# New instruction orders on TensorE, ScalarE and VectorE in a fused layernorm, linear attention and FFN kernel

## The chip, the cores and the metric

The kernel runs on one core of a Trainium2 chip. The metric is the device time of one execution in microseconds (us). Three executions of the kernel before took 555.29, 557.46 and 555.6 us, median 555.6 us. All times in the text are us unless marked ns.

## The reference

The input x has 8 batches of 1024 tokens with 256 channels. The output is x + attention + FFN, both of the layernorm of x:

```
xn  = layernorm(x)
q, k, v = split(xn @ qkv_w + qkv_b), 16 heads of 16 channels
q = q / |q| ; k = k / |k|            (per token and head)
kv  = sum over tokens of k^T v       (16x16 per head)
att = (q @ kv) @ proj_w + proj_b
ffn = relu(xn @ W1 + b1) @ W2 + b2   (1024 hidden channels)
out = x + att + ffn
```

## The kernel before

All matrix products are done in three passes of rounded float32: each operand is held as a rounded high part and a low part (the rest), and a product is high x high, high x low, low x high. So every operand costs a high part (a copy, mostly on ScalarE: functions *_high) and a low part (a subtraction, mostly on VectorE: *_low; for the normalised rows on GpSimd: split_xn).

A batch b is two halves of 512 tokens, s = 2b (even) and 2b + 1 (odd). In a half, TensorE runs the FFN as eight pairs ffn_up(s, u, j) (512 columns, six matmuls, into w_bank[j % 2]) and ffn_down(s, b, u, j) (six matmuls of 512 columns into o_bank). I call each such group of six a unit. ffn_up(j) may start when h_low(j - 2) has emptied its bank; ffn_down(j) needs h_low(j). h_high(s, j) on ScalarE and h_low(s, j) on VectorE turn the bank into the two parts of the hidden rows.

Between the units stand the products of attention, most of them short (256 or 128 columns): gather (xn^T k, eight matmuls of 512 columns and eight of 256), key_value, project, and the query-key product of the next half. That is done for two tile pairs n = 0, 1 in four steps, qk_begin (six matmuls of 256), qk_second (six), qk_third (six), qk_fourth (three), with fewer products in all than the plain form. Between the steps ScalarE and VectorE pass partial sums on: qk_seed on ScalarE (two copies of 256 columns; it waits for qk_begin and for both outputs of the pair before, qk_pair_out), qk_seed on VectorE (needed by qk_third), qk_sum on VectorE (needed by qk_fourth). qk_pair_out (a square and a copy) empties the banks; its second call for a pair waits for qk_fourth. Then sum_pair_squares, bound, qk_root and norms give 1/|q|, 1/|k|; divide(1, u) scales k and divide(0, u) scales q, and the high and low parts follow. At the end of a batch attend multiplies q with the batch's matrix m (m_high, m_low), and yT_out, add_attention, spread_y and GpSimd's add_rows build the output rows.

Transposes go by VectorE in 32x32 blocks (transpose_x, transpose_q) and then by 16 DMAs that SyncE issues (move). When the x blocks of half s + 1 have landed (x_moved), GpSimd forms three sums of them (x_forms, lines 445, 449 and 452; they are the input of the query-key steps), and ScalarE copies them (xT_high).

Each engine works through its own list in order; the lists are written out by hand: second_half (the odd half of batch 0), even_half and odd_half (batches 1 to 6 and the even half's and odd half's order in a loop), last_even_half and last_odd_half (batch 7). Engines meet by semaphores only. An instruction that waits holds up all that stands behind it in its list. The odd half's first TensorE units before are up 2, up 3, down 0, down 1, down 2, up 4.

Of the kernel before, what the change touches and what calls it, by code (L numbers as in the profile page):

```python
# [66 lines left out]
def build(nc, x, qkv_w, qkv_b, proj_w, proj_b, w1, b1, w2, b2, out):  # L67
# [6 lines left out]
    with ctx:  # L74
# [895 lines left out]
        def _(dve):  # L970
# [340 lines left out]
            def even_half(b, s):  # L1311
# [62 lines left out]
            def last_even_half(b, s):  # L1374
                h_low(s, 2)
                xT_low(s + 1, 1)
                x_forms_low(s + 1)
# [6 lines left out]
                h_low(s, 5)
                transpose_q(s, 0)
                k_low(s, 0)
                h_low(s, 6)
                qk_seed(s + 1, 1)
# [508 lines left out]
```

## Time and profile before

| | before |
|---|---|
| median of three executions | 555.6 us (555.29 to 557.46) |
| the profiled execution, its span | 555.33 us, 553.6 us |
| granted TensorE clock | 1.00 of full speed all along |
| TensorE busy | 546.7 us (99%), 2824 matmuls |
| weight loads busy | 466.2 us (84%) |
| VectorE, ScalarE, GpSimd busy | 441.4 us (80%), 311.6 us (56%), 188.4 us (34%) |

The page's busy time of TensorE counts each matmul from its start to its modelled end; they overlap, so the distance from start to start is what counts for the time. In the timelines each line has the start and the duration in us.

### The profile page before, as it was taken

To read this page: it belongs to the slowest core of one execution; us is meant where nothing else is said; L and a number is where in the kernel's file an instruction comes from. 1 tells how busy PE (TensorE), PEld (TensorE's weight loads), DVE (VectorE), ACT (ScalarE), POOL (GpSimd) and SP (SyncE) were. 2 spreads that over 40 slices of the span, in tenths; PEclk is the share of its full clock that TensorE was granted. 3 is DMA by queue.
4 is the path that set the end of the run, shared out by engine and by line. 5 is a ranking of instruction groups with operands and counts; after the bars stand their busy time and mean duration, and the time that the engine had idled before them with its cause. 6 is when DMAs were issued, how large, how long until landed. Compare 5 with 4: busy or idle time off the path is not lost.

```text
span 553.6 us, 9454 instructions
## 1 busy us (share of the span) xinstructions
PE 546.7 (99%) x2824; PEld 466.2 (84%) x2824; DVE 441.4 (80%) x856; ACT 311.6 (56%) x594; POOL 188.4 (34%) x196
## 2 busy tenths in 40 slices
PE   9999999999999999999999999999999999999997
PEld 7888878878888788887988888888888888888896
DVE  6977799687896878879698697977879778785745
ACT  4686644674636665475744757547484473743520
POOL 4242678140370304622146222442226331270010
PEclk9999999999999999999999999999999999999999
DMA  8522134351432525135251352413524133140633
GB/s 260 167 84 50 38 85 88 79 108 42 103 61 76 108 71 106 23 78 109 71 100 29 79 108 71 92 38 81 105 71 85 38 72 79 36 78 18 136 76 78
DMA packets 141416, 45.37 MB, mean 82 GB/s; under 512 B 133331, under 2 KB 136403, under 8 KB 141397
## 3 DMA queue, kind: packets, MB, share of 16 engines
q1 hardware_dynamic: 139280, 44.61, 35.1%
q10 hardware_dynamic: 2116, 0.53, 0.5%
q8 instruction: 9, 0.15, 0.1%
q14 instruction: 11, 0.08, 0.1%
HBM read 20.98 MB, written 8.39 MB: 53 GB/s over the span
## 4 chain that ended last, share of the span: by engine, by line
PE 88%; DVE 8%; issue 2%; ACT 1%; DVEq 0%
PE o_bank L1453 11%; PE o_bank L1454 10%; PE o_bank L1455 10%; PE w_bank L1453 9%; PE w_bank L1454 9%; PE w_bank L1455 9%; PE v_bank L1453 6%; PE v_bank L1455 6%; PE v_bank L1454 6%; DVE w_raw L1145 4%; PE g_bank L1629 3%; PE kv_bank L1629 3%; DVE h_lo L1159 1%; PE kv_bank L1634 1%; PE g_bank L1634 1%
## 5 line engine op out<-in xcount | busy, mean ns | idle before, releaser
L719 ACT ACTIVATE h_hi<-w_bank 128x512 fp32r<-128x512 f32 x128 | 75.9, 599 | 89.7 <-PE w_bank L1455 89.6
L438 POOL TENSOR_TENSOR xn_lo<-xn,xn_hi 128x256 fp32r<-128x256 f32 x56 | 42.1, 751 | 191.8 <-ACT xn_hi L598 187.6
L1453 PE MATMUL w_bank<-xT_hi,w_hi 128*128 128x512 f32 x254 | 100.1, 394 | 0.0
L1454 PE MATMUL w_bank<-xT_lo,w_hi 128*128 128x512 f32 x254 | 99.4, 391 | 0.0
L1455 PE MATMUL w_bank<-xT_hi,w_lo 128*128 128x512 f32 x254 | 99.0, 390 | 0.0
L1453 PE MATMUL o_bank<-h_hi,w_hi 128*128 128x512 f32 x240 | 94.9, 395 | 1.4 <-DVE h_lo L1159 1.4
L1454 PE MATMUL o_bank<-h_lo,w_hi 128*128 128x512 f32 x240 | 94.1, 392 | 0.0
L1455 PE MATMUL o_bank<-h_hi,w_lo 128*128 128x512 f32 x240 | 93.4, 389 | 0.0
L1159 DVE SCALAR_TENSOR_TENSOR h_lo<-w_bank,h_hi 128x512 fp32r<-128x512 f32 x128 | 86.2, 682 | 6.5 <-ACT h_hi L719 4.1
L486 POOL TENSOR_TENSOR y_sb<-y_sb,y_rows 128x256 f32<-128x256 f32 x56 | 63.3, 1135 | 13.8 <-DVE y_rows L1203 10.5
L1455 PEld LDWEIGHTS w_bank<-xT_hi,w_lo 128*128 128x128 f32 x254 | 47.7, 188 | 10.5
L1453 PEld LDWEIGHTS w_bank<-xT_hi,w_hi 128*128 128x128 f32 x254 | 47.8, 188 | 9.7 <-DVE h_lo L1159 1.2
L1453 PEld LDWEIGHTS o_bank<-h_hi,w_hi 128*128 128x128 f32 x240 | 45.3, 189 | 11.3 <-DVE h_lo L1159 4.0
L1454 PEld LDWEIGHTS w_bank<-xT_lo,w_hi 128*128 128x128 f32 x254 | 47.9, 188 | 8.0
L1455 PEld LDWEIGHTS o_bank<-h_hi,w_lo 128*128 128x128 f32 x240 | 45.1, 188 | 9.9
L1454 PEld LDWEIGHTS o_bank<-h_lo,w_hi 128*128 128x128 f32 x240 | 45.3, 189 | 7.0
L1126 DVE TENSOR_REDUCE qk_v<-qk_sq 128x32 f32<-128x512 f32 x52 | 35.2, 676 | 12.7 <-ACT qk_sq L700 12.7
L445 POOL TENSOR_TENSOR xn<-xT_raw 128x512 f32<-128x512 f32 x13 | 18.2, 1400 | 64.1 <-DMA xT_raw<-blocks 64.1
L1116 DVE TENSOR_TENSOR v_bank<-v_bank,qk_fifth 128x256 f32<-128x256 f32 x26 | 11.2, 432 | 34.2 <-PE v_bank L1455 34.2
L625 ACT ACTIVATE xn<-x_sb,ln_offset,ln_rstd 128x256 f32<-128x256 f32 x52 | 27.0, 591 | 20.2 <-DVE ln_offset L1034 20.2
L700 ACT ACTIVATE qk_sq<-v_bank 128x512 f32<-128x512 f32 x52 | 31.0, 595 | 9.1 <-DVE v_bank L1121 6.5
L1145 DVE TENSOR_TENSOR w_raw<-w_raw,qk_rn 128x1024 f32<-128x1024 f32 x16 | 25.6, 1631 | 0.1
(246 smaller groups left out, 1253.5 us busy)
## 6 DMA issues: line engine op xcount, KB each, us to landing
y_rows<-blocks SPq DMA_DIRECT2D x256, 32.0 KB, 1.9
x_sb<-x SPq DMA_DIRECT2D x15, 512.0 KB, 3.4
y_sb<-x SPq DMA_DIRECT2D x60, 128.0 KB, 3.2
out<-y_sb SPq DMA_DIRECT2D x58, 128.0 KB, 2.5
xT_raw<-blocks SPq DMA_DIRECT2D x224, 32.0 KB, 1.9
y_sb<-w SPq DMA_DIRECT2D x4, 256.0 KB, 5.3
x_sb<-x SPq DMA_DIRECT2D x2, 256.0 KB, 3.0
w_raw<-w SPq DMA_DIRECT2D x2, 256.0 KB, 7.4
```

Source lines behind the costliest of these rows:

```text
L438: nc.gpsimd.tensor_tensor(xn_lo[:, u, t, :], xn_of(s)[:, t, :], xn_hi[:, u, t, :].bitcast(F32), ALU.subtract).then_inc(xn_split_done, 1)
L486: nc.gpsimd.tensor_tensor(y_sb[:, u, t, :], y_sb[:, u, t, :], y_rows[:, u, t, :], ALU.add).then_inc(y_done, 1)
L625: done = nc.scalar.activation(to[:, t, :], x_sb[:, u, t, :], ACT.Identity, bias=ln_offset[:, t:t + 1], scale=ln_rstd[:, t:t + 1])
L700: nc.scalar.activation(qk_sq[:, w, :], v_bank[w][:], ACT.Square).then_inc(qk_sq_done, 1)
L719: nc.scalar.activation(h_hi[:, j % RING, :], w_bank[j % 2][:], ACT.Relu).then_inc(h_done, 1)
L1126: nc.vector.tensor_reduce(to, qk_sq[:, w, :].rearrange("p (w h d) -> p w h d", w=2, d=D), AXIS.X, ALU.add).then_inc(qk_ss_done, 1)
L1145: nc.vector.tensor_tensor(part, part, by, ALU.mult).then_inc(done, 1)
L1159: nc.vector.scalar_tensor_tensor(h_lo[:, r, :], w_bank[j % 2][:], 0.0, h_hi[:, r, :].bitcast(F32), ALU.max, ALU.subtract).then_inc(h_lo_do ...
L1453: nc.tensor.matmul(to, left[0], right[0], start=first, stop=False, skip_group_check=shared)
L1454: nc.tensor.matmul(to, left[0], right[1], start=False, stop=False, skip_group_check=shared)
L1455: return nc.tensor.matmul(to, left[1], right[0], start=False, stop=last, skip_group_check=shared)
L1629: nc.tensor.matmul(g_banks[k][:], xn_hi[:, u, t, k * P:(k + 1) * P], k_parts[:, t].rearrange("p w n -> p (w n)"), start=u == 0 and t == 0, ...
```

## The change

Only the order of the calls in the hand-written lists of TensorE, ScalarE and VectorE changes, in second_half, even_half, odd_half, last_even_half and last_odd_half. No instruction is added or taken away, no size, wait or buffer is changed, and GpSimd's and SyncE's lists stay as they are. In the odd half TensorE's first units become up 2, down 0, down 1, up 3, up 4, down 2; in the even half up 2, down 0, down 1, up 3, down 2, up 4. The short groups come side by side more often (gather with qk_begin, qk_fourth with qk_begin, key_value between qk_second and qk_third). The diff, function by function, with the calls alone (the two lists of the last batch, changed in the same way, are left out):

```diff
# scalar: second_half
...
+h_high(1, 3)
 xn_high(2, 0)
-h_high(1, 3)
+ln_root(3)
 k_high(1, 1)
-ln_root(3)
+qk_out(2, 0, 0)
+qT_high(0, 0)
+qk_out(2, 0, 1)
 normalise(3, 1)
+g_high(0)
 h_high(1, 4)
-qk_out(2, 0, 0)
+qk_out(2, 0, 2)
+h_high(1, 5)
 xn_high(3, 1)
-qT_high(0, 0)
-h_high(1, 5)
-g_high(0)
-qk_out(2, 0, 1)
 h_high(1, 6)
-qk_out(2, 0, 2)
 h_high(1, 7)
-qT_high(1, 1)
 qk_out(2, 0, 3)
 h_high(2, 0)
+qT_high(1, 1)
 m_high(0)
# scalar: even_half
...
 h_high(s, 4)
-h_high(s, 5)
 qk_seed(s + 1, 0)
 ln_root(s + 2)
+h_high(s, 5)
 normalise(s + 2, 0)
 qk_pair_out(s + 1, 1, 0, 0)
+xn_high(s + 2, 0)
 qk_pair_out(s + 1, 1, 0, 1)
 qk_seed(s + 1, 1)
+qT_high(s, 0)
 h_high(s, 6)
 h_high(s, 7)
-qT_high(s, 0)
-xn_high(s + 2, 0)
 qk_pair_out(s + 1, 1, 1, 0)
 qk_pair_out(s + 1, 1, 1, 1)
+h_high(s + 1, 0)
 qk_root(s + 1)
-h_high(s + 1, 0)
-h_high(s + 1, 1)
 yT_out(b, 0, 0)
 yT_out(b, 0, 1)
+h_high(s + 1, 1)
 xT_high(s + 2, 0)
# scalar: odd_half
...
 g_high(b)
-qk_seed(s + 1, 0)
 ln_root(s + 2)
 h_high(s, 4)
+qk_seed(s + 1, 0)
 h_high(s, 5)
...
 qk_pair_out(s + 1, 0, 0, 0)
+h_high(s, 6)
+xn_high(s + 2, 1)
 qk_pair_out(s + 1, 0, 0, 1)
 qk_seed(s + 1, 1)
-xn_high(s + 2, 1)
-h_high(s, 6)
-qT_high(s, 1)
 h_high(s, 7)
...
 qk_pair_out(s + 1, 0, 1, 0)
+qk_pair_out(s + 1, 0, 1, 1)
 h_high(s + 1, 0)
-qk_pair_out(s + 1, 0, 1, 1)
+qk_root(s + 1)
+qT_high(s, 1)
 h_high(s + 1, 1)
-qk_root(s + 1)
 xT_high(s + 2, 1)
# vector: second_half
...
 transpose_q(1, 1)
+sum_squares(2, 0)
 h_low(1, 3)
+transpose_x(3)
 h_low(1, 4)
-g_low(0)
-transpose_x(3)
-h_low(1, 5)
-sum_squares(2, 0)
-h_low(1, 6)
 sum_squares(2, 1)
 qT_low(0, 0)
+h_low(1, 5)
+g_low(0)
 sum_squares(2, 2)
+h_low(1, 6)
 mask_kv(0)
...
 sum_squares(2, 3)
+m_low(0)
 bound(2)
 h_low(2, 0)
-m_low(0)
 h_low(2, 1)
# vector: even_half
...
 transpose_q(s, 0)
+xT_low(s + 1, 1)
+h_low(s, 3)
 x_forms_low(s + 1)
-h_low(s, 3)
-xT_low(s + 1, 1)
 variance(s + 2, b + 1, 0)
+h_low(s, 4)
+spread(s + 2)
 qk_seed(s + 1, 0)
-spread(s + 2)
-h_low(s, 4)
+qk_sum(s + 1, 0)
+transpose_x(s + 2)
 h_low(s, 5)
-qk_sum(s + 1, 0)
 sum_pair_squares(s + 1, 0, 0)
-transpose_x(s + 2)
+qk_seed(s + 1, 1)
 sum_pair_squares(s + 1, 0, 1)
-qk_seed(s + 1, 1)
 h_low(s, 6)
+h_low(s, 7)
+qk_sum(s + 1, 1)
 qT_low(s, 0)
-qk_sum(s + 1, 1)
-h_low(s, 7)
 sum_pair_squares(s + 1, 1, 0)
...
 h_low(s + 1, 0)
+divide(1, 1, k_done)
 h_low(s + 1, 1)
-divide(1, 1, k_done)
# vector: odd_half
...
 divide(0, 1, q_done)
+h_low(s, 2)
 transpose_q(s, 1)
-h_low(s, 2)
 k_low(s, 1)
+xT_low(s + 1, 0)
+h_low(s, 3)
 x_forms_low(s + 1)
-h_low(s, 3)
-xT_low(s + 1, 0)
 variance(s + 2, b + 1, 1)
+spread(s + 2)
 g_low(b)
+qk_seed(s + 1, 0)
 h_low(s, 4)
-qk_seed(s + 1, 0)
-spread(s + 2)
 h_low(s, 5)
 qk_sum(s + 1, 0)
+mask_kv(b)
 transpose_x(s + 2)
-mask_kv(b)
+sum_pair_squares(s + 1, 0, 0)
+h_low(s, 6)
+sum_pair_squares(s + 1, 0, 1)
 qk_seed(s + 1, 1)
-h_low(s, 6)
+h_low(s, 7)
 qk_sum(s + 1, 1)
-sum_pair_squares(s + 1, 0, 0)
-h_low(s, 7)
-sum_pair_squares(s + 1, 0, 1)
 m_low(b)
-qT_low(s, 1)
 sum_pair_squares(s + 1, 1, 0)
-h_low(s + 1, 0)
 sum_pair_squares(s + 1, 1, 1)
 bound(s + 1)
+h_low(s + 1, 0)
 norms(s + 1)
+qT_low(s, 1)
 h_low(s + 1, 1)
# tensor: second_half
...
 ffn_up(1, 1, 2)
+ffn_down(1, 0, 1, 0)
 ffn_up(1, 1, 3)
-ffn_down(1, 0, 1, 0)
 query_key(2, 0, 0)
+query_key(2, 0, 1)
 ffn_down(1, 0, 1, 1)
-query_key(2, 0, 1)
 ffn_up(1, 1, 4)
...
 gather(1, 0, 1)
+query_key(2, 0, 2)
 ffn_up(1, 1, 5)
...
 ffn_down(1, 0, 1, 3)
-query_key(2, 0, 2)
+ffn_up(1, 1, 7)
 ffn_down(1, 0, 1, 4)
-ffn_up(1, 1, 7)
 key_value(0)
+query_key(2, 0, 3)
+ffn_up(2, 0, 0)
 ffn_down(1, 0, 1, 5)
-ffn_up(2, 0, 0)
-query_key(2, 0, 3)
-ffn_down(1, 0, 1, 6)
 project(0)
 ffn_up(2, 0, 1)
+ffn_down(1, 0, 1, 6)
 ffn_down(1, 0, 1, 7)
# tensor: even_half
...
 ffn_up(s, 0, 2)
-ffn_up(s, 0, 3)
 ffn_down(s, b, 0, 0)
 ffn_down(s, b, 0, 1)
+ffn_up(s, 0, 3)
+ffn_down(s, b, 0, 2)
 ffn_up(s, 0, 4)
 gather(s, b, 0)
+qk_begin(s + 1, 1, 0, b)
 ffn_up(s, 0, 5)
-qk_begin(s + 1, 1, 0, b)
-ffn_down(s, b, 0, 2)
 qk_second(s + 1, 1, 0)
+ffn_up(s, 0, 6)
+qk_third(s + 1, 0)
 ffn_down(s, b, 0, 3)
-qk_third(s + 1, 0)
-ffn_up(s, 0, 6)
+ffn_down(s, b, 0, 4)
 qk_fourth(s + 1, 1, 0)
+qk_begin(s + 1, 1, 1, b)
 ffn_up(s, 0, 7)
-qk_begin(s + 1, 1, 1, b)
-ffn_down(s, b, 0, 4)
 qk_second(s + 1, 1, 1)
...
 qk_third(s + 1, 1)
+ffn_up(s + 1, 1, 0)
+qk_fourth(s + 1, 1, 1)
 ffn_down(s, b, 0, 6)
-qk_fourth(s + 1, 1, 1)
-ffn_up(s + 1, 1, 0)
 ffn_up(s + 1, 1, 1)
# tensor: odd_half
...
 ffn_up(s, 1, 2)
-ffn_up(s, 1, 3)
 ffn_down(s, b, 1, 0)
 ffn_down(s, b, 1, 1)
+ffn_up(s, 1, 3)
+ffn_up(s, 1, 4)
 ffn_down(s, b, 1, 2)
-ffn_up(s, 1, 4)
 gather(s, b, 1)
 qk_begin(s + 1, 0, 0, b)
+ffn_up(s, 1, 5)
 ffn_down(s, b, 1, 3)
-ffn_up(s, 1, 5)
 qk_second(s + 1, 0, 0)
+key_value(b)
+qk_third(s + 1, 0)
 ffn_up(s, 1, 6)
-qk_third(s + 1, 0)
+ffn_up(s, 1, 7)
+qk_fourth(s + 1, 0, 0)
+qk_begin(s + 1, 0, 1, b)
 ffn_down(s, b, 1, 4)
-qk_fourth(s + 1, 0, 0)
-key_value(b)
-qk_begin(s + 1, 0, 1, b)
-ffn_up(s, 1, 7)
 qk_second(s + 1, 0, 1)
...
 qk_fourth(s + 1, 0, 1)
+ffn_up(s + 1, 0, 1)
 ffn_down(s, b, 1, 6)
-ffn_up(s + 1, 0, 1)
 ffn_down(s, b, 1, 7)
...
```

## Rows read from the trace of the kernel before

**Rows 1.** List of waits, TensorE: total us, times, longest.
```profile
PE o_bank L1453 <- DVE h_lo L1159: 1.4, 6, 0.3
```

**Rows 2.** Timeline of TensorE around a gather: short and long products.
```profile
263.17 0.28 PE L1453 MATMUL v_bank<-wqk_hi,xT_hi 128*128 128x256 f32 x1
...
263.89 0.40 PE L1453 MATMUL o_bank<-h_hi,w_hi 128*128 128x512 f32 x1
...
265.28 0.39 PE L1453 MATMUL w_bank<-xT_hi,w_hi 128*128 128x512 f32 x1
...
266.64 0.28 PE L1453 MATMUL v_bank<-wqk_forms_hi,xf_hi 128*128 128x256 f32 x1
```

**Rows 3.** Timeline of TensorE at the start of an odd half: start, duration, line, operation.
```profile
251.61 0.44 PE L1453 MATMUL w_bank<-xT_hi,w_hi 128*128 128x512 f32 x1
253.05 0.39 PE L1453 MATMUL w_bank<-xT_hi,w_hi 128*128 128x512 f32 x1
...
256.90 0.39 PE L1455 MATMUL o_bank<-h_hi,w_lo 128*128 128x512 f32 x1
257.53 0.50 PE L1453 MATMUL o_bank<-h_hi,w_hi 128*128 128x512 f32 x1 [0.24 <-DVE h_lo L1159]
...
259.02 0.40 PE L1453 MATMUL w_bank<-xT_hi,w_hi 128*128 128x512 f32 x1
```

**Rows 4.** Timeline of VectorE there: last of norms, h_low 0 and 1, both divides, h_low 2.
```profile
250.38 0.29 DVE L983 SCALAR_TENSOR_TENSOR qk_rn<-qk_e,qk_y 128x128 f32<-128x128 f32 x1
250.81 1.29 DVE L1159 SCALAR_TENSOR_TENSOR h_lo<-w_bank,h_hi 128x512 fp32r<-128x512 f32 x2
252.01 3.45 DVE L1145 TENSOR_TENSOR w_raw<-w_raw,qk_rn 128x1024 f32<-128x1024 f32 x2
...
256.82 0.65 DVE L1159 SCALAR_TENSOR_TENSOR h_lo<-w_bank,h_hi 128x512 fp32r<-128x512 f32 x1
```

**Rows 5.** Timeline of the weight loads there.
```profile
251.55 0.19 PEld L1453 LDWEIGHTS w_bank<-xT_hi,w_hi 128*128 128x128 f32 x1 [0.20 <-DVE h_lo L1159]
```

**Rows 6.** VectorE's block transposes of x, even half before rows 3.
```profile
240.11 1.30 DVE L1068 STREAM_TRANSPOSE blocks<-xn 128x512 f32<-128x512 f32 x2
```

**Rows 7.** Timeline of ScalarE, same half: yT_out twice.
```profile
251.13 1.40 ACT L733 ACTIVATE xn_first<-o_bank,bias_T 128x512 f32<-128x512 f32 x2
```

**Rows 8.** Timeline of ScalarE: qk_seed's two copies; the last copy of qk_pair_out.
```profile
241.84 0.37 ACT L598 ACTIVATE v_bank<-v_bank 128x256 f32<-128x256 f32 x1 [0.91 <-PE v_bank L1455]
242.12 0.38 ACT L598 ACTIVATE qk_fifth<-v_bank 128x256 f32<-128x256 f32 x1
...
248.20 0.59 ACT L598 ACTIVATE w_raw<-v_bank 128x512 f32<-128x512 f32 x1
```

**Rows 9.** TensorE: the qk_fourth whose result that last copy takes.
```profile
247.15 0.28 PE L1453 MATMUL v_bank<-wqk_forms_hi,xT_hi 128*128 128x256 f32 x1
```

**Rows 10.** The divide's line, one of its two forms: duration in ns, least, median, most.
```profile
L1145 DVE TENSOR_TENSOR w_raw<-w_raw,qk_rn x16: 1211/1220/2327, 53.7 to 523.2; 128x1024 f32<-128x1024 f32 x16
```

**Rows 11.** Timeline of GpSimd in the stretch of rows 3.
```profile
253.07 1.31 POOL L445 TENSOR_TENSOR xn<-xT_raw 128x512 f32<-128x512 f32 x1 [4.17 <-DMA xT_raw<-blocks]
254.46 1.60 POOL L449 TENSOR_TENSOR xn<-xT_raw,xn 128x256 f32<-128x256 f32 x1
```

**Rows 12.** SyncE's moves of x in the even half before rows 3.
```profile
241.43 10.28 SPq L372 DMA_DIRECT2D xT_raw<-blocks  x16
```

**Rows 13.** TensorE at the end of batch 0: attend starts late.
```profile
82.01 0.47 PE L1453 MATMUL v_bank<-qT_hi,m_hi 128*128 128x512 f32 x1 [0.83 <-issue]
```

**Rows 14.** VectorE there: bound, h_low, m_low, and qT_low.
```profile
78.47 2.24 DVE L1132 TENSOR_SCALAR qk_v<-qk_v 128x128 f32<-128x128 f32 x1
...
81.24 0.67 DVE L973 TENSOR_TENSOR m_lo<-g_bank,m_hi 128x512 fp32r<-128x512 f32 x1
...
83.40 1.23 DVE L973 TENSOR_TENSOR qT_lo<-y_rows,qT_hi 128x1024 fp32r<-128x1024 f32 x1
```

**Rows 15.** GpSimd there: the low parts of the weight forms.
```profile
78.24 2.40 POOL L471 TENSOR_TENSOR wqk_forms_lo<-wvp_raw,wqk_forms_hi 128x1024 fp32r<-128x1024 f32 x1
```

More of the change, by code:

```diff
@@ L898, in odd_half @@
                 qk_pair_out(s + 1, 0, 1, 0)
+                qk_pair_out(s + 1, 0, 1, 1)
                 h_high(s + 1, 0)
-                qk_pair_out(s + 1, 0, 1, 1)
+                qk_root(s + 1)
+                qT_high(s, 1)
                 h_high(s + 1, 1)
-                qk_root(s + 1)
                 xT_high(s + 2, 1)
             def last_even_half(b, s):
+                x_forms_high(s + 1)
                 h_high(s, 2)
+                h_high(s, 3)
+                qk_seed(s + 1, 0)
+                h_high(s, 4)
+                h_high(s, 5)
                 k_high(s, 0)
-                x_forms_high(s + 1)
-                h_high(s, 3)
-                h_high(s, 4)
-                qk_seed(s + 1, 0)
-                h_high(s, 5)
                 qk_pair_out(s + 1, 1, 0, 0)
+                h_high(s, 6)
                 qk_pair_out(s + 1, 1, 0, 1)
-                h_high(s, 6)
+                qk_seed(s + 1, 1)
                 h_high(s, 7)
-                qk_seed(s + 1, 1)
+                qk_pair_out(s + 1, 1, 1, 0)
                 h_high(s + 1, 0)
-                qk_pair_out(s + 1, 1, 1, 0)
                 qk_pair_out(s + 1, 1, 1, 1)
                 qk_root(s + 1)
-                h_high(s + 1, 1)
                 qT_high(s, 0)
                 yT_out(b, 0, 0)
+                h_high(s + 1, 1)
                 yT_out(b, 0, 1)
@@ L931, in last_odd_half @@
                 h_high(s, 4)
+                g_high(b)
                 h_high(s, 5)
-                g_high(b)
+                m_high(b)
                 h_high(s, 6)
-                m_high(b)
                 qT_high(s, 1)
@@ L1315, in even_half @@
                 transpose_q(s, 0)
+                xT_low(s + 1, 1)
+                h_low(s, 3)
                 x_forms_low(s + 1)
-                h_low(s, 3)
-                xT_low(s + 1, 1)
                 variance(s + 2, b + 1, 0)
+                h_low(s, 4)
+                spread(s + 2)
                 qk_seed(s + 1, 0)
-                spread(s + 2)
-                h_low(s, 4)
+                qk_sum(s + 1, 0)
+                transpose_x(s + 2)
                 h_low(s, 5)
-                qk_sum(s + 1, 0)
                 sum_pair_squares(s + 1, 0, 0)
-                transpose_x(s + 2)
+                qk_seed(s + 1, 1)
                 sum_pair_squares(s + 1, 0, 1)
-                qk_seed(s + 1, 1)
                 h_low(s, 6)
+                h_low(s, 7)
+                qk_sum(s + 1, 1)
                 qT_low(s, 0)
-                qk_sum(s + 1, 1)
-                h_low(s, 7)
                 sum_pair_squares(s + 1, 1, 0)
@@ L1374, in last_even_half @@
             def last_even_half(b, s):
+                xT_low(s + 1, 1)
                 h_low(s, 2)
-                xT_low(s + 1, 1)
+                h_low(s, 3)
                 x_forms_low(s + 1)
-                h_low(s, 3)
+                divide(0, 0, q_done)
+                h_low(s, 4)
                 qk_seed(s + 1, 0)
-                h_low(s, 4)
-                divide(0, 0, q_done)
+                h_low(s, 5)
                 qk_sum(s + 1, 0)
+                transpose_q(s, 0)
+                h_low(s, 6)
+                h_low(s, 7)
+                qk_seed(s + 1, 1)
                 sum_pair_squares(s + 1, 0, 0)
[L1384 to L1388, printed above, removed]
                 qk_sum(s + 1, 1)
                 sum_pair_squares(s + 1, 0, 1)
-                h_low(s, 7)
+                k_low(s, 0)
                 sum_pair_squares(s + 1, 1, 0)
@@ L1396, in last_even_half @@
                 h_low(s + 1, 0)
+                divide(1, 1, k_done)
                 h_low(s + 1, 1)
-                divide(1, 1, k_done)
                 qT_low(s, 0)
@@ L1403, in last_odd_half @@
                 divide(0, 1, q_done)
+                k_low(s, 1)
+                transpose_q(s, 1)
                 h_low(s, 3)
-                transpose_q(s, 1)
-                k_low(s, 1)
+                h_low(s, 4)
                 g_low(b)
-                h_low(s, 4)
                 mask_kv(b)
@@ L1412, in last_odd_half @@
                 m_low(b)
+                qT_low(s, 1)
                 h_low(s, 7)
-                qT_low(s, 1)
             def half(b, s, u, last):
@@ L1810, in last_even_half @@
                 ffn_up(s, 0, 2)
+                ffn_up(s, 0, 3)
                 ffn_down(s, b, 0, 0)
-                ffn_up(s, 0, 3)
                 ffn_down(s, b, 0, 1)
+                ffn_down(s, b, 0, 2)
+                qk_begin(s + 1, 1, 0, b)
                 ffn_up(s, 0, 4)
-                qk_begin(s + 1, 1, 0, b)
-                ffn_down(s, b, 0, 2)
+                ffn_down(s, b, 0, 3)
                 qk_second(s + 1, 1, 0)
@@ L1819, in last_even_half @@
                 qk_third(s + 1, 0)
-                ffn_down(s, b, 0, 3)
-                qk_fourth(s + 1, 1, 0)
                 ffn_up(s, 0, 6)
                 ffn_up(s, 0, 7)
+                qk_fourth(s + 1, 1, 0)
                 qk_begin(s + 1, 1, 1, b)
                 ffn_down(s, b, 0, 4)
+                ffn_up(s + 1, 1, 0)
+                qk_second(s + 1, 1, 1)
                 ffn_down(s, b, 0, 5)
-                qk_second(s + 1, 1, 1)
+                qk_third(s + 1, 1)
                 ffn_down(s, b, 0, 6)
-                qk_third(s + 1, 1)
-                ffn_up(s + 1, 1, 0)
                 qk_fourth(s + 1, 1, 1)
+                ffn_up(s + 1, 1, 1)
                 gather(s, b, 0)
-                ffn_up(s + 1, 1, 1)
                 ffn_down(s, b, 0, 7)
@@ L1837, in last_odd_half @@
                 ffn_up(s, 1, 2)
-                ffn_up(s, 1, 3)
                 ffn_down(s, b, 1, 0, True)
                 ffn_down(s, b, 1, 1, True)
+                ffn_up(s, 1, 3)
                 ffn_up(s, 1, 4)
-                ffn_up(s, 1, 5)
                 gather(s, b, 1)
                 ffn_down(s, b, 1, 2, True)
+                ffn_up(s, 1, 5)
+                ffn_up(s, 1, 6)
+                key_value(b)
                 ffn_down(s, b, 1, 3, True)
-                key_value(b)
-                ffn_up(s, 1, 6)
                 ffn_down(s, b, 1, 4, True)
                 project(b)
+                ffn_down(s, b, 1, 5, True)
                 ffn_up(s, 1, 7)
-                ffn_down(s, b, 1, 5, True)
                 attend_first(s, b)
```

2 lines of the change are left out of this document (1 added, 1 removed).

## The prediction

> **What bounds the kernel now.** I read the page first: TensorE is busy for 99% of the span at full granted clock, and the weight loads for 84%, and no other engine is above 80%. TensorE's busy share includes overlap, so the second view is its list of waits: VectorE's h_lo held it up 6 times [rows 1], once in each of batches 1 to 6. The third view is the timeline, from start to start. An undisturbed unit of six long matmuls takes 266.64 - 265.28 = 1.36, one behind short products 265.28 - 263.89 = 1.39, six short ones 263.89 - 263.17 = 0.72 [rows 2]. Everything on TensorE is such units laid end to end, so time can only be won where a start is late or where a neighbour costs extra. The late start is in the odd half: ffn_down 2 starts 0.63 after the last matmul before it, where 0.23 is the pace, and takes 259.02 - 257.53 = 1.49 to the end of the unit instead of 1.36 [rows 3]. That is 0.40 + 0.13 = 0.53 in a batch, 3.2 in six. Its cause is VectorE's list: h_low 2 starts at 256.82 behind two divides and a transpose [rows 4]. A second late start, at the end of batch 0, is in part 5.
>
> **Part 1: the wait of ffn_down 2 (odd half, six times).** Let T = 251.57 be the start of the odd half in the new order (251.61 less what part 2 takes from the half before). Up 2 takes 253.05 - 251.61 = 1.44 [rows 3], since its first weight load was late by a little [rows 5]; I leave that as it is. h_low 2 is now needed first by up 4, the fifth unit, at T + 1.44 + 3 x 1.36 = 257.1, with its weight load 0.23 earlier, 256.9. On VectorE it moves ahead of the transpose (1.31, as in [rows 6]) but one divide moves ahead of h_low 1. If nothing collides, h_low 0 ends at 251.5, the divide at 252.7, h_low 1 follows ScalarE, the second divide follows, and h_low 2 ends before 256. So the wait goes, and what is late next is h_low 1: ffn_down 1 is now the third unit, due at T + 1.44 + 1.36 = 254.37, and ScalarE makes h_high 1 only behind the two yT_out that end at 252.53 [rows 7], so at about 253.1; h_low 1 (0.69) ends at 253.8 at best. Cover 0.5. Value: -0.53 x 6 = -3.2. Bounds: 0 (a new wait of the same size) and -3.2.
>
> **Part 2: short groups side by side.** A group of shorts costs 1.39 - 1.36 = 0.03 on the unit behind it, and gives back a little under 0.01 at its own start; I take 0.02 for each group that vanishes. An even half has 9 groups before and 7 after, an odd half 6 and 5; over six batches 18, and 2 in the last batch: -0.4. Bounds: 0 and 20 x 0.03 = -0.6. The Trainium skill ("TensorE: Matmul & The Clock Gate", section "Back-to-back issue gap") gives a spacing that depends on the matmul's own columns, 131 ns at 512, with no term for the neighbour; by it this part is worth 0. The rows differ from it in both: 227 ns a long matmul and 0.03 for a short neighbour [rows 2].
>
> **Part 3: the seed before qk_second of the second pair (12 times).** New order: fourth, begin, one up or down, second; before there was one unit more between. Let F be the start of qk_fourth. The last copy that waits for it ends at F + (248.79 - 247.15) = F + 1.64 [rows 8, 9]. qk_seed's two copies take 242.50 - 241.84 = 0.66 [rows 8], with hand-overs of 0.03 on both sides: F + 2.36. Due is F + 0.36 + 0.71 + 1.39 = F + 2.46, its weight load 0.23 earlier. So the load starts late but the matmul nearly in time, as in [rows 5], where a load 0.06 ahead of its matmul cost 0.05 to 0.08. I take 0.05 x 12 = +0.6. Bounds: 0, and 0.2 x 12 = +2.4 if ScalarE comes to the pair output 0.15 late (in the odd half xn_high, a copy of 1.07, now stands ahead of it and by my sum ends only 0.13 before it is due).
>
> **Part 4: the divide against GpSimd's sums (six times).** A divide takes 1.22 alone and 2.33 at most [rows 10]; the second of the two in [rows 4] ends at 255.46, 1.08 after GpSimd's first sum ended (253.07 + 1.31) [rows 11], and GpSimd's second sum, on half the columns of the first, took 1.60 and not some 0.7. So whichever starts first holds the other up wholly. The page "SBUF — State Buffer" of the Trainium skill, section "Who interferes with whom", says the same of a VectorE operation with both inputs in SBUF: the first to issue takes the shared pair for its whole length. That rule speaks against this change, by the following count from rows. The divide is meant to come before the sums, but the sums move too: in the even half transpose_x goes up to right behind qk_sum 0. From the end of qk_third 0 to T there are d3, d4, fourth, begin, up 7, second, d5, third, up 0, fourth, d6, up 1, d7: 2 x 0.36 + 3 x 0.71 + 5 x 1.39 + 3 x 1.36 = 13.9. So its last result is there at 237.8, qk_sum (a 256-column addition, estimated at 0.35 from the copies of 256 columns in [rows 8]) and the transposes (1.30) end at 239.5 instead of 241.41 [rows 6], and the blocks land 253.07 - 241.43 = 11.64 later [rows 11, 12], at 251.15. GpSimd's first sum then runs from 251.2 to 252.5, and the divide, free to start at 251.4 behind h_low 0, waits for it: end 252.5 + 1.08 = 253.6, h_low 1 at 254.2, its weight load at 254.27, 0.1 before ffn_down 1 is due. As in [rows 5] that costs about 0.05. The second divide meets the next sum (some 0.7) and ends near 255.45, h_low 2 near 256.1, still 0.8 before 256.9. Value 0.05 x 6 = +0.3. Bounds: 0 (the divide is first) and 0.5 x 6 = +3.
>
> **Part 5: the end of batch 0.** attend stands 0.83 idle, 0.99 by starts (a long matmul of 0.39 overlaps the next by 0.16), and 0.08 in its first matmul, behind m_low [rows 13, 14]. m_low stood behind bound, which took 2.24 for 128 columns, since GpSimd held it off until 80.64 [rows 14, 15], and behind h_low. Now m_low is ahead of bound and attend can start on time. But its second half needs qT_low of the odd half, which ended at 84.63 [rows 14] behind the same bound: without m_low's 0.6 in front it ends near 84.0 to 84.2, when TensorE, unstalled, wants it at 82.01 - 0.99 + 2 x 1.36 = 83.74. So -0.5 is left of 1.07. On the way there h_low 5 now stands behind qT_low(0, 0), which meets GpSimd's proj_lo; the wait of about 0.5 that I expect there falls into the same slack. Bounds: +0.3 and -1.07.
>
> **Elsewhere** nothing is on the path. These are sums of the same unit times against the lists in the diff, rough to 0.2: gather still finds k_low a microsecond early, key_value (moved forward) comes 0.8 behind g_low, qk_third 0.6 behind its seed, up 6 0.6 behind h_low 4, up 0 of the next half 0.5 behind h_low 6. In the last batch I expect no stall above 0.1. SyncE issues the same DMAs; the moves of x in the even half start 1.9 earlier, when its queue is free.
>
> **Sum.** -3.2 - 0.4 + 0.6 + 0.3 - 0.5 = -3.2 on the profiled execution, 555.33 to 552.1. The median of three is 0.27 above that execution, so 555.6 - 3.2 = 552.4.
>
> **Rivals.**
> A, all covers hold: seeds and divides cost nothing (parts 3 and 4 at 0). -3.2 - 0.4 - 0.5 = -4.1: 551.5. For it: the steps that are moved had 0.4 and more to spare. Against: the covers I count are 0.1.
> B, the wait only changes its name: h_low 1, or the seed, is late by about 0.4 a batch, because the divide has gone ahead of it and meets a sum. Then parts 1 and 4 give -0.1 x 6, and the rest -0.3: -1.0, 554.6. For it: six small covers of 0.1 to 0.8 in a row, each worked out to 0.1 or so.
> C, slower: GpSimd's first sum lands on norms. The last of norms' three small operations (0.29) ends at 250.67, just before h_low 0 [rows 4], and up 2 waits for h_low 0 already [rows 5]. If the blocks land before 250.7 instead of 251.15, the sum (1.31) holds norms and h_low 0 up, up 2 starts 1.2 late, and ffn_down 1 another 0.1 to 0.5 late behind the divide: +1.2 + 0.3 - 0.53 - 0.06 = +0.9 a batch, +5.5 in six, less the 0.5 of part 5: 560.6. It decides at 0.45 of my count of the transposes. bound in [rows 14] shows the like. Against: my count would have to be off by three times its roughness, and the transposes also need xn_done, which ScalarE's list gives only about 0.3 before.
>
> **Chances.** Forecast 0.50, with its own range 551.6 to 553.3; A 0.17; B 0.26; C 0.07. A measurement of this kernel can tell about 0.5%, 2.8 us, from no change, so faster means under 552.8. That holds A and some four fifths of the forecast: 0.58. The same holds the rest of the forecast and B less a little: 0.35; slower 0.07. The range runs from 551.0 (A with its bounds) to 555.2 (B), C left out.
>
> **What would show it.** In the new profile: no wait of an o_bank matmul on h_lo L1159 in the odd half, so none 6 times in the list of waits; each batch is 0.4 to 0.5 shorter. The divide that writes w_raw ahead of h_low 1 takes 2.3 if GpSimd is first, 1.2 if not. The first matmul of the second qk_second comes 0.00 to 0.1 late. attend of batch 0 has a gap of at most 0.6, and not before its first half. The prediction is wrong if a wait of 0.3 or more turns up six times at another place, or if the batch is not shorter by at least 0.3.

## Result and the profile after

| | before | after |
|---|---|---|
| median, first comparison | 555.99 us (555.29 to 557.46, 4 runs) | 551.5 us (551.1 to 552.07, 4 runs) |
| ratio, 95% interval | | 0.9917, 0.9894 to 0.994 |
| the profiled execution, its span | 555.33, 553.6 us | 551.33, 549.6 us |
| second comparison (run x2 below) | 555.14 us (9 runs) | 551.12 us (5 runs), ratio 0.9927, 0.9914 to 0.9941 |
| third comparison (x9 to x11 below) | 555.14 us (17 runs) | |

The change makes the kernel 0.7 to 0.8% faster, 4.0 to 4.5 us. The prediction was 552.4 (551.0 to 555.2). Of the 17 executions in the third comparison one took 1404.83 us; the ratios leave it out.

The page after, its busy times:

```profile
span 549.6 us, 9448 instructions
PE 544.7 (99%) x2824; PEld 465.4 (85%) x2824; DVE 437.9 (80%) x856; ACT 313.2 (57%) x594; POOL 189.1 (34%) x196
```

The list of waits after, TensorE's matmuls, to be laid beside [rows 1]:

```profile
PE w_bank L1685 <- DVE xT_raw L1220: 1.1, 1, 1.1
PE w_bank L1453 <- DVE h_lo L1159: 0.2, 1, 0.2
```

The first line, a wait in the opening, stood in the list before too. The six waits of o_bank on h_lo are gone; one of w_bank is new (batch 0, below). The weight loads show what the matmuls' own list hides:

```profile
PEld v_bank L1453 <- ACT qk_fifth L598: 2.3, 12, 0.2
PEld w_bank L1453 <- DVE h_lo L1159: 1.9, 7, 0.7
```

The first line is the seed of part 3, twelve times as forecast.

TensorE's timeline after at the start of the same odd half, against [rows 3]:

```profile
249.75 0.44 PE L1453 MATMUL w_bank<-xT_hi,w_hi 128*128 128x512 f32 x1
...
251.18 0.39 PE L1453 MATMUL o_bank<-h_hi,w_hi 128*128 128x512 f32 x1
...
252.55 0.39 PE L1453 MATMUL o_bank<-h_hi,w_hi 128*128 128x512 f32 x1
...
253.91 0.39 PE L1453 MATMUL w_bank<-xT_hi,w_hi 128*128 128x512 f32 x1
...
255.27 0.39 PE L1453 MATMUL w_bank<-xT_hi,w_hi 128*128 128x512 f32 x1
```

These are the first matmuls of up 2, down 0, down 1, up 3 and up 4. Apart from up 2 (1.43 instead of 1.36) every unit takes 1.36 or 1.37: no matmul waits there.

VectorE and GpSimd there, against [rows 4] and [rows 11]:

```profile
248.94 0.69 DVE L1159 SCALAR_TENSOR_TENSOR h_lo<-w_bank,h_hi 128x512 fp32r<-128x512 f32 x1
249.55 2.17 DVE L1145 TENSOR_TENSOR w_raw<-w_raw,qk_rn 128x1024 f32<-128x1024 f32 x1
251.64 0.68 DVE L1159 SCALAR_TENSOR_TENSOR h_lo<-w_bank,h_hi 128x512 fp32r<-128x512 f32 x1
252.24 1.21 DVE L1145 TENSOR_TENSOR w_raw<-w_raw,qk_rn 128x1024 f32<-128x1024 f32 x1
253.37 0.68 DVE L1159 SCALAR_TENSOR_TENSOR h_lo<-w_bank,h_hi 128x512 fp32r<-128x512 f32 x1
```

```profile
249.34 1.29 POOL L445 TENSOR_TENSOR xn<-xT_raw 128x512 f32<-128x512 f32 x1 [7.42 <-DMA xT_raw<-blocks]
250.71 1.61 POOL L449 TENSOR_TENSOR xn<-xT_raw,xn 128x256 f32<-128x256 f32 x1
252.40 1.65 POOL L452 TENSOR_TENSOR xn<-xT_raw,xn 128x256 f32<-128x256 f32 x1
```

GpSimd is first by 0.2, and the divide is held as part 4 expected. h_low 2 (the fifth line) is done at 254.05, for a weight load at 255.04.

**Where the 4 us come from.** A batch is measured from the start of attend's second half to the next one, on the profiled executions. Its length is called the period below; for the runs it is the median of batches 1 to 6.

| stretch | before | after | difference |
|---|---|---|---|
| start to the 101st matmul | 23.36 | 23.10 | -0.26 |
| from there to attend's second half of batch 0 | 61.48 | 60.99 | -0.49 |
| batches 1 to 6, each | 67.15 | 66.60 | -0.55, six times -3.30 |
| last batch, to the last matmul | 62.12 | 62.09 | -0.03 |

The last matmul starts 4.09 earlier; the whole span is 4.0 shorter. The first row is not the change's doing: over the thirteen profiled executions, all with the same lists up to there, the 101st matmul started between 22.70 and 23.42, and two executions of the changed kernel's best variant (x3 and x11 below) stand at 22.70 and 23.25. Single times therefore differ by up to 0.7 for nothing. The period is steadier: within one execution of the kernel before or after, the six batches agree within 0.05, and a second execution of the same kernel has the same mean to 0.02 (66.60 twice; 66.55 and 66.53 for x3 and x11). The verdicts below go by it. In x3 to x6, x9 and x10 batch 1 alone differs from the other five by 0.12 to 0.31, which the median leaves out. Five runs (x4 to x8) were executed once each, so that their times by themselves say less than their periods.

### The profile page after: what moved, and what is told of

Same layout as the page of the kernel before. It is cut to its first block, busy times and chain, and to the rows that moved or that the text cites. A ratio compares the mean times of both kernels' runs of the same rounds, so it can differ in the third digit from the quotient of the medians.

```text
span 549.6 us, 9448 instructions
## 1 busy us (share of the span) xinstructions
PE 544.7 (99%) x2824; PEld 465.4 (85%) x2824; DVE 437.9 (80%) x856; ACT 313.2 (57%) x594; POOL 189.1 (34%) x196
## 4 chain that ended last, share of the span: by engine, by line
PE 91%; SPq 4%; ACT 3%; DVE 1%; issue 1%; DMA 0%; ACTq 0%
PE o_bank L1453 11%; PE o_bank L1454 11%; PE o_bank L1455 11%; PE w_bank L1453 10%; PE w_bank L1454 10%; PE w_bank L1455 10%; PE v_bank L1453 6%; PE v_bank L1455 6%; PE v_bank L1454 6%; SPq L372 4%; PE kv_bank L1629 2%; PE g_bank L1629 2%; PE kv_bank L1634 1%; PE g_bank L1634 1%; PE kv_bank L1647 1%; PE w_bank L1685 1%
## 5 line engine op out<-in xcount | busy, mean ns | idle before, releaser
L1453 PE MATMUL o_bank<-h_hi,w_hi 128*128 128x512 f32 x240 | 93.8, 391 | 0.0
L1116 DVE TENSOR_TENSOR v_bank<-v_bank,qk_fifth 128x256 f32<-128x256 f32 x26 | 11.2, 432 | 24.0 <-PE v_bank L1455 23.8
L1121 DVE TENSOR_TENSOR v_bank<-v_bank,qk_fifth 128x256 f32<-128x256 f32 x26 | 11.2, 432 | 21.8 <-PE v_bank L1455 21.8
```

The lines of the kernel that those rows point to most:

```text
L1453: nc.tensor.matmul(to, left[0], right[0], start=first, stop=False, skip_group_check=shared)
```

## The experiments

Each edit is in the engines' lists alone, and each diff is against the kernel that its name says.

**x1, one edit of the change, on the kernel before.** VectorE, odd half:

```diff
 divide(0, 1, q_done)
+h_low(s, 2)
 transpose_q(s, 1)
-h_low(s, 2)
```

> The kernel before with one call moved: in VectorE's odd half, h_low 2 ahead of the transposes of q. Theory (the wait of ffn_down 2 was the bulk of the gain): h_low 2 ends near 256.05 on the scale of the old profile instead of 257.47, ffn_down 2 is due at 257.13, so the six waits go: batch period 67.15 to 66.62, total -3.2 us, about 552.4. Rival (the gain needs TensorE's new order of units): the wait stays or moves to gather, which needs k_low; then less than -1 us.

Measured: 551.77 (551.68 to 552.55, 5 runs), ratio 0.9944 (0.993 to 0.9957); period 66.607. All six waits are gone, and no other of h_lo has come to the matmuls' list. One line moved past another gives 0.55 of the 0.55 a batch. All other new orders in the six batches together move the period by less than 0.01 (means of the six 66.603 in x1, 66.601 and 66.600 in the two profiled executions of the changed kernel), which is no more than the scatter.

**x2, the changed kernel again**, in the same comparison:

> The changed kernel once more, to stand beside the others on one chip: 551.5 within 0.5, about 0.992 of the kernel before.

Measured: 551.12 (550.86 to 551.22), period 66.61. Against x1 it is 0.65 better, about what the end of batch 0 is worth (x7).

**x4, the reverse of x1 on the changed kernel**: h_low 2 goes back behind transpose_q.

```diff
 divide(0, 1, q_done)
-h_low(s, 2)
 transpose_q(s, 1)
+h_low(s, 2)
```

> The changed kernel with h_low 2 of the odd half behind the transposes again, as it was before. Theory (TensorE's new unit order does not move the due time of h_low 2; both orders need it as fifth unit): h_low 2 ends at T + 5.5, its weight load is due at T + 5.3, so up 4 comes 0.1 to 0.2 late, less than the old 0.53 because the divides are now 0.9 earlier behind h_low 1: +0.6 to +1.2 us in six batches. Rival (the divides' new place does not count): the full wait is back, +3.2 us.

Measured, one run: 553.61, period 66.98, so +0.38 a batch: more than the theory's 0.1 to 0.2 and less than the rival's 0.53. In batch 1 the period is only 66.71. The place is up 4, on TensorE and VectorE:

```profile
322.60 0.39 PE L1455 MATMUL w_bank<-xT_hi,w_lo 128*128 128x512 f32 x1
323.06 0.50 PE L1453 MATMUL w_bank<-xT_hi,w_hi 128*128 128x512 f32 x1
323.40 0.39 PE L1454 MATMUL w_bank<-xT_lo,w_hi 128*128 128x512 f32 x1
```

```profile
321.12 1.31 DVE L1068 STREAM_TRANSPOSE blocks<-w_raw 128x512 f32<-128x512 f32 x2
322.35 0.65 DVE L1159 SCALAR_TENSOR_TENSOR h_lo<-w_bank,h_hi 128x512 fp32r<-128x512 f32 x1
```

0.46 - 0.23 = 0.23 of lateness and 0.34 - 0.23 = 0.11 in the matmul behind it make 0.34 of the 0.38. h_low 2 ends at 323.00, and up 4 needs the bank that it empties. So with every other new order in place the batch is only 67.15 - 66.98 = 0.17 shorter than before; the move of h_low 2 alone takes all 0.55.

**x6, the divide behind h_low 1 again**, on the changed kernel, VectorE, even half:

```diff
 h_low(s + 1, 0)
-divide(1, 1, k_done)
 h_low(s + 1, 1)
+divide(1, 1, k_done)
```

> The changed kernel with the divide of k in the even half behind h_low 1 again, where it was before. Theory (the divide's place is worth next to nothing as long as h_low 1 is in time): h_low 1 is limited by ScalarE and ends 0.5 earlier; the divides meet GpSimd's third sum instead, h_low 2 ends 1.5 to 1.7 later than in the changed kernel, just when up 4 is due; 0 to 0.1 a batch, 0 to +0.6 us. Rival (moving the divide is what freed h_low 2): the old wait is back, 0.4 or more a batch, +2.4 us.

Measured, one run: 552.65, period 66.83, +0.23 a batch, between the two expectations. Its VectorE and GpSimd one batch later than the stretch above:

```profile
318.40 0.69 DVE L1159 SCALAR_TENSOR_TENSOR h_lo<-w_bank,h_hi 128x512 fp32r<-128x512 f32 x1 [1.54 <-ACT h_hi L719]
319.01 2.71 DVE L1145 TENSOR_TENSOR w_raw<-w_raw,qk_rn 128x1024 f32<-128x1024 f32 x2
```

```profile
316.58 1.30 POOL L445 TENSOR_TENSOR xn<-xT_raw 128x512 f32<-128x512 f32 x1 [7.46 <-DMA xT_raw<-blocks]
317.95 0.73 POOL L449 TENSOR_TENSOR xn<-xT_raw,xn 128x256 f32<-128x256 f32 x1
318.76 0.74 POOL L452 TENSOR_TENSOR xn<-xT_raw,xn 128x256 f32<-128x256 f32 x1
```

With the divide no longer ahead of them the second and third sums take 0.73 and 0.74 instead of 1.61 and 1.65, but VectorE idles 1.54 for ScalarE. All that it does afterwards is about 1.0 later, counted from the half's start (h_low 2 starts at T + 4.67 instead of T + 3.62, T being the start of up 2), and 13 us on that reaches TensorE: g_parts are done at 332.23, key_value's first weight load is due at 332.05.

```profile
332.29 0.19 PEld L1647 LDWEIGHTS kv_bank<-g_parts,wv_hi 128*128 128x128 f32 x1 [0.17 <-DVE g_parts L1168]
```

0.23 is lost there in this batch. So the early divide pays although it is held up for a microsecond: it uses time in which VectorE would wait for ScalarE.

**x5, the groups of the even half set apart**, on the changed kernel, TensorE:

```diff
 gather(s, b, 0)
-qk_begin(s + 1, 1, 0, b)
 ffn_up(s, 0, 5)
-qk_second(s + 1, 1, 0)
+qk_begin(s + 1, 1, 0, b)
 ffn_up(s, 0, 6)
-qk_third(s + 1, 0)
+qk_second(s + 1, 1, 0)
 ffn_down(s, b, 0, 3)
+qk_third(s + 1, 0)
 ffn_down(s, b, 0, 4)
 qk_fourth(s + 1, 1, 0)
```

> The changed kernel with TensorE's even half from gather to qk_fourth in another order: gather, up 5, begin, up 6, second, down 3, third, down 4, fourth, so that qk_begin stands apart from gather; one more group of short products in each of six even halves, all else equal. Theory (a group costs by its edges): each even half 0.02 to 0.03 longer, +0.15 in all, seen in the distance of the batches. Rival (the page's rule, spacing by the matmul's own columns): 0.00. qk_third comes 1.36 later, so the transposes of x and GpSimd's first sum do too, and by the lock the divide ahead of h_low 1 then takes 1.2 instead of 2.2, with no change of TensorE's time.

Measured, one run: 555.94, period 67.33, +0.73 a batch: a plain miss. The edit did not only part two groups, it left one unit instead of two between qk_third and qk_fourth. ScalarE in that stretch, and the matmul that waits:

```profile
307.59 0.59 ACT L598 ACTIVATE w_raw<-v_bank 128x512 f32<-128x512 f32 x1
308.06 1.06 ACT L598 ACTIVATE xn_hi<-xn 128x1024 fp32r<-128x1024 f32 x1
309.01 0.60 ACT L700 ACTIVATE qk_sq<-v_bank 128x512 f32<-128x512 f32 x1
309.49 0.61 ACT L598 ACTIVATE w_raw<-v_bank 128x512 f32<-128x512 f32 x1
310.13 0.37 ACT L598 ACTIVATE v_bank<-v_bank 128x256 f32<-128x256 f32 x1
310.41 0.38 ACT L598 ACTIVATE qk_fifth<-v_bank 128x256 f32<-128x256 f32 x1
```

```profile
310.21 0.40 PE L1455 MATMUL w_bank<-xT_hi,w_lo 128*128 128x512 f32 x1
310.85 0.39 PE L1453 MATMUL v_bank<-wqk_forms_hi,xf_hi 128*128 128x256 f32 x1 [0.24 <-ACT qk_fifth L598]
```

qk_fourth is done at 308.24, but ScalarE's square starts at 309.01, behind xn_hi's 1.06. qk_second starts 0.41 late and loses 0.10 more in its first matmul; qk_begin ahead of it waits for the copy that ends at 308.18, 0.25 in all the same way. 0.51 + 0.25, less the 0.03 that the changed kernel loses there anyway, is the 0.73 to within 0.02. The question that the run was built for, what one group more costs, is drowned by this.

**x9, x5 with xn_high behind the seed**, ScalarE:

```diff
 qk_pair_out(s + 1, 1, 0, 0)
-xn_high(s + 2, 0)
 qk_pair_out(s + 1, 1, 0, 1)
 qk_seed(s + 1, 1)
+xn_high(s + 2, 0)
 qT_high(s, 0)
```

> The run with the groups of the even half set apart (x5) and one more move: ScalarE's xn_high stands behind the second pair's seed, not ahead of it. Theory: x5 lost 0.49 a batch because only one long unit was left between qk_third and qk_fourth of the first pair, so the pair output of qk_fourth met xn_high (1.06) on ScalarE and the seed's copies came 0.4 late. Then this kernel gets that back, about 2.9 in six batches, and stands 1.2 to 1.8 above the changed kernel (0.13 a batch for qk_begin, which still waits for a copy of the pair output, and three more short groups at 0.025 each): 552.3 to 553.0. Rival: separated groups themselves cost that much, or the later xn_high makes the blocks of the next x late: then it stays at 555 or above.

Measured: 554.16 (553.97 to 554.75, 12 runs), ratio 0.9982 (0.9973 to 0.999); period 67.09. qk_second is on time again, so xn_high was the cause of its wait: 0.49 a batch come back. But 0.25 go again, which neither expectation had: xn_high and qT_high now run one after the other just ahead of h_high 6 and 7 (ScalarE starts on those two at 311.31), and up 0 waits for h_low 6.

```profile
312.43 0.28 PE L1455 MATMUL v_bank<-wqk_forms_hi,xf_lo 128*128 128x256 f32 x1
312.69 0.50 PE L1453 MATMUL w_bank<-xT_hi,w_hi 128*128 128x512 f32 x1
```

Take the measured stalls away (0.25 at qk_begin, 0.25 here, less 0.03) and 0.02 of the 0.49 above the changed kernel is left for the one group more that this order has, a remainder that is rough to 0.01.

**x7, second_half (batch 0) of all three engines as before**, the rest as changed:

> The changed kernel with the lists of batch 0's odd half (second_half on TensorE, ScalarE and VectorE) as they were before. Theory: the first o_bank matmul of attend in batch 0 is 0.5 later, all later batches as in the changed kernel: +0.5 us. Rival (batch 0's end gives the lead back later in waits): 0.

Measured, one run: 551.76; from the 101st matmul to attend's second half 61.54, against 60.99 and 60.95 in two executions of the changed kernel and 61.48 before. The other runs have the one or the other list of batch 0 and agree: 61.52 with the old one (x1), 60.73 to 60.97 with the new one (x4, x5, x6, x8, x9). Part 5 is worth 0.5 to 0.8, on its own. Which of the moves in these lists does it no run tells; the trace after has m_low done at 78.78, 2.6 ahead of attend, where before it stood last ahead of it.

**x8, h_low 0 ahead of norms**, on the changed kernel, VectorE, even half:

```diff
 bound(s + 1)
-norms(s + 1)
 h_low(s + 1, 0)
+norms(s + 1)
 divide(1, 1, k_done)
```

> The changed kernel with h_low 0 of the next half ahead of norms in the even half, alone. Theory: first weight load of up 2 in time, 0.08 a batch, -0.5 us; the divide ahead of h_low 1 takes 1.2, since it starts before GpSimd's first sum. Rival (the load's lateness is free): batch distance unchanged at 66.58.

Measured, one run: 550.87, period 66.53, -0.07 a batch. up 2's late weight load ([rows 5]), which the change had left, is gone: it starts at 249.22 for a matmul at 249.44. And here the divide comes first, at 248.72, and GpSimd is the one that is held:

```profile
248.72 1.22 DVE L1145 TENSOR_TENSOR w_raw<-w_raw,qk_rn 128x1024 f32<-128x1024 f32 x1
```

```profile
249.02 2.08 POOL L445 TENSOR_TENSOR xn<-xT_raw 128x512 f32<-128x512 f32 x1 [7.43 <-DMA xT_raw<-blocks]
```

**x3 and x11, x8 and h_low 5 ahead of qT_low in batch 0**, VectorE, second_half:

```diff
 sum_squares(2, 1)
-qT_low(0, 0)
 h_low(1, 5)
+qT_low(0, 0)
 g_low(0)
```

> The changed kernel with two calls moved on VectorE: in the even half h_low 0 of the next half ahead of norms instead of behind it, and in batch 0 h_low 5 ahead of qT_low(0, 0). Theory: up 2 of the odd half no longer waits for h_low 0 (0.08 a batch), the divide starts before GpSimd's first sum and takes 1.2 instead of 2.2, which gains nothing on TensorE, and batch 0 loses its wait of 0.50 at up 7 but gets 0.2 to 0.3 of it back as a wait of attend for qT_low. Sum -0.5 - 0.25 = -0.75 us against the changed kernel, 550.7. Rival (the late weight load costs nothing, since TensorE makes it up): only batch 0's 0.25.

> The best version so far (x3) once more, on the same chip as x10: 550.2, within 0.4.

Measured: 550.19 (549.93 to 550.64) with ratio 0.991 (0.9895 to 0.9925), and 550.14 (550.09 to 550.44) with ratio 0.9906 (0.9891 to 0.9922). It is faster than both kernels (555.14 and, in the same comparison as x3, 551.12). In batch 0 its two profiled executions take 60.95 and 60.44, where x8 takes 60.93: nothing in the one and 0.5 in the other. Whether the move of h_low 5 earns the 0.5 isn't shown, since the 60.44 goes with a chance of another kind. VectorE's bound in x3, then in x11:

```profile
77.77 2.43 DVE L1132 TENSOR_SCALAR qk_v<-qk_v 128x128 f32<-128x128 f32 x1
```

```profile
78.31 0.21 DVE L1132 TENSOR_SCALAR qk_v<-qk_v 128x128 f32<-128x128 f32 x1
```

GpSimd's subtraction of 2.40 starts at 77.72 in x3, 0.05 ahead of bound, and at 78.35 in x11, 0.04 behind its start; there the small operation behind bound and two h_low is held instead, until 80.93, and qT_low ends at 82.85 instead of 83.51. In x3 qT_low then ends late, and attend's second half starts 0.50 late:

```profile
83.65 0.47 PE L1453 MATMUL o_bank<-qT_hi,m_hi 128*128 128x512 f32 x1 [0.34 <-DVE qT_lo L973]
```

**x10, the kernel before with four moves only**: second_half as in x3, h_low 2 as in x1, h_low 0 as in x8. All other orders in the six batches and the last are those of before.

> The kernel before with only these: second_half of all three engines as in the changed kernel with h_low(1, 5) ahead of qT_low(0, 0); VectorE's h_low 2 ahead of transpose_q in the odd half; VectorE's h_low(s+1, 0) ahead of norms in the even half. All other orders are those of before. Theory: of the change only the wait in the odd half and the end of batch 0 carry its gain, the merged groups (-0.08 a batch) and the later seeds (+0.06) cancel, so the time equals that of the best version so far (x3, 550.2) within 0.4. Rival: the other new orders are worth something in six batches (merged groups without their cost): then this one is 0.5 or more above x3.

Measured: 550.54 (550.31 to 551.13, 6 runs), ratio 0.9914 (0.99 to 0.9929). In medians it is 0.35 above x3 and 0.40 above x11, at the edge of what was expected. In spite of the run's name these are not four calls: two calls are moved in the six batches, and the lists of batch 0's odd half are new on three engines. The period is 66.527, that of x3 to the last digit (66.526 to 66.534 in x11). In the profiled executions x10 loses 0.56 to x11 in batch 0 (61.00 against 60.44: two stalls of 0.26 and 0.35, at attend's second half and 18 us ahead of it) and 0.12 in batch 1, and has 0.43 less before the 101st matmul; where the medians' 0.40 lies is not shown. Its weight loads never wait for a seed.

## Why the prediction was right, and where it was not

The forecast had the place of the gain, its cause and nearly its size; its central number was 0.9 to 1.3 too high. Its own range, 551.6 to 553.3, misses the measured 551.5 and 551.12 by 0.1 and 0.5.

**Part 1** (-3.2) was right in place and size: x1 shows it alone at -0.55 a batch with no new wait, though its own sum gave 0.53. The sign that the prediction named, a batch 0.4 to 0.5 shorter, was passed at 0.55. That the first cover to fail would be thin was right too: h_low 1 ends at 252.32, its weight load starts at 252.37, and down 1 is on time.

**Part 2** (-0.4) fits, but no run has it alone. x1 and the changed kernel differ by less than 0.01 a batch. The changed kernel has two late seeds (2 x 0.028) and three groups fewer, so a group is worth 0.056 / 3 = 0.019 if nothing else differs. The remainder in x9 is 0.02 too. Both speak against the 0 that the prediction works out for a spacing without a term for the neighbour. That parts 2 and 3 cancel in a batch (-0.06 against +0.06) was not foreseen.

**Part 3** (+0.6) had the right place and count, but the size was off: a late load ahead of a 256-column matmul costs 0.028, not the 0.05 that I took from a 512-column one, so +0.33:

```profile
307.58 0.19 PEld L1453 LDWEIGHTS v_bank<-wqk_forms_hi,xf_hi 128*128 128x128 f32 x1 [0.19 <-ACT qk_fifth L598]
```

```profile
307.65 0.31 PE L1453 MATMUL v_bank<-wqk_forms_hi,xf_hi 128*128 128x256 f32 x1
307.80 0.28 PE L1454 MATMUL v_bank<-wqk_forms_lo,xf_hi 128*128 128x256 f32 x1
```

The matmul is in time, and the one behind it comes 0.15 later instead of 0.12 (over all kept traces the cost is 0.026 to 0.034). The case of its upper bound (0.2 each, "if ScalarE comes to the pair output 0.15 late") was real, and worse than the bound: x5 loses 0.49 at that place from one unit less.

**Part 4** (+0.3) had the mechanism right to 0.04. GpSimd's first sum starts 0.41 ahead of T (forecast 0.37), the divide ends 1.09 behind the sum's end (1.08 in [rows 4, 11]), and h_low 1 at T + 2.57 (forecast T + 2.6). The price was wrong. The load is 0.18 ahead of its matmul, and that costs nothing, where 0.06 ahead costs 0.05 to 0.08. The traces show it in both directions: the divide is held in the changed kernel (2.17 instead of 1.22), the sum in x8 (2.08 instead of 1.29). The Trainium skill's rule that the first to start keeps the pair of ports for its whole length ("SBUF — State Buffer", section "SBUF: two separate sides") agrees with them. What I had not weighed is that the held time was idle time: x6 shows that leaving the divide behind costs 0.23.

**Part 5** (-0.5) was right in size (-0.49). In the changed kernel's first profile the rest of the stall shows at another place than I had said. attend is unstalled in both halves:

```profile
81.37 0.39 PE L1453 MATMUL v_bank<-qT_hi,m_hi 128*128 128x512 f32 x1
...
84.09 0.40 PE L1453 MATMUL o_bank<-qT_hi,m_hi 128*128 128x512 f32 x1
```

The loss stands 13 us earlier, at up 7, behind h_low 5, which stands behind the held qT_low(0, 0):

```profile
65.86 2.16 DVE L973 TENSOR_TENSOR qT_lo<-y_rows,qT_hi 128x1024 fp32r<-128x1024 f32 x1
67.94 0.68 DVE L1159 SCALAR_TENSOR_TENSOR h_lo<-w_bank,h_hi 128x512 fp32r<-128x512 f32 x1
```

```profile
68.05 0.39 PE L1455 MATMUL o_bank<-h_hi,w_lo 128*128 128x512 f32 x1
68.67 0.50 PE L1453 MATMUL w_bank<-xT_hi,w_hi 128*128 128x512 f32 x1 [0.23 <-DVE h_lo L1159]
```

0.39 of lateness and 0.11 in the matmul make 0.50. But the place is not the kernel's own. x4, x5, x6, x8 and x9 have the same lists in batch 0. In x8 and x9 the wait stands at up 7 as here, and in x2 it is spread over up 7 and a unit 3 us ahead. In x4, x5 and x6 qT_low(0, 0) is not held, GpSimd's proj_lo is, and the wait stands at attend's second half, with up to 0.58, just where the prediction had it. So it is in x5:

```profile
65.74 1.21 DVE L973 TENSOR_TENSOR qT_lo<-y_rows,qT_hi 128x1024 fp32r<-128x1024 f32 x1
```

```profile
65.73 2.38 POOL L562 TENSOR_TENSOR proj_lo<-wvp_raw,proj_hi 128x512 fp32r<-128x512 f32 x1
```

```profile
84.13 0.47 PE L1453 MATMUL o_bank<-qT_hi,m_hi 128*128 128x512 f32 x1 [0.34 <-DVE qT_lo L973]
```

The sentence that the wait of h_low 5 "falls into the same slack" holds: with it or without it the stretch is about as long (60.99 here, 60.93 in x5 and 60.95 in x3). Only in x11, where bound escapes GpSimd, are both gone. The sign that I named, a gap at attend, is thus a sign of some executions only.

**The sum.** Forecast -3.2, profiled -4.09 up to the last matmul. Of the 0.9 between them 0.27 are the seeds, 0.3 the divide, 0.26 the opening's scatter, and 0.07 parts 1, 2 and the last batch together. By its parts this is rival A (551.5: seeds and divides cost nothing, for which 0.33 is still too little), which had 0.17. I gave covers of 0.1 too high a price. The 0.26 of the opening is chance, and no part of the change. Rival B, the wait that only changes its name, did not happen; x5 shows how near it was, one unit away. Rival C did not happen either: the first sum started 249.34 - 248.81 = 0.53 behind the end of norms' last operation, where I had counted 0.48.

## What to carry to other kernels

When all engines' lists change at once, look for the single wait that the old profile names, and try the one move that ends it on the old kernel: here one line gave 0.55 of 0.55 us a batch. Two moved calls in the loop and new lists for batch 0's odd half gave at least as much as the whole change (x10, 550.54 against 551.12; its moves of h_low 0 and h_low 5 are not in the change). The other orders were neutral together, and they took away cover: twelve weight loads wait for a seed that don't in x10. With them in place a harmless-looking reordering (x5) cost 4.6 us; whether it would have cost that on the kernel before wasn't tried. Price a late start by how far the weight load runs ahead of its matmul, not by whether a wait is listed. When an operation is held by another engine, ask what its engine would otherwise have done in that time. And before a wait is taken for a kernel's own, look for it in a second execution.

## What the runs showed of the hardware

- A weight load that starts 0.18 ahead of its matmul instead of 0.23 costs nothing (down 1 in the changed kernel, 1.36); 0.06 to 0.07 ahead costs 0.05 to 0.08 before 512 columns (up 2; x8 wins 0.07 by ending it) and about 0.03 before 256 (the seeds). When the matmul itself is late, the one behind it loses about 0.1 more (0.11 in x4 and x9, 0.10 in x5).
- Which of VectorE and GpSimd is held turned on a few hundredths, and came out both ways for the same lists. In batch 0 qT_low(0, 0) was held in x9 (starts 0.02 apart) and proj_lo in x5 (0.01 apart), with the same lists there, and TensorE's wait stood 15 us further on in x5. bound was held in x3 (2.43) and not in x11 (0.21), one and the same kernel, and batch 0 was 0.5 shorter.
- A group of short matmuls between long ones costs about 0.02 us beyond its own length, by [rows 2] and by what is left over in x9 and between x1 and the changed kernel. Kinds of groups were not told apart.
